# Half-row maximum tiles in pairs, after the four scores of a chunk, in a fused eight-block transformer kernel on one Trainium2 core

## The reference

```
x = x + slot_attention(layernorm(x))       # 4 heads, 64 slots, causal
x = x + mixture_of_low_rank_experts(layernorm(x))
x = x + polar_attention(layernorm(x))      # 16 heads of 8: "L0_attn_b"
x = x + mixture_of_low_rank_experts(layernorm(x))
x = x + distance_attention(layernorm(x))   # 16 heads of 8: "L1_attn_a"
x = x + squared_relu_ffn(layernorm(x))
x = x + gated_attention(layernorm(x))      # 16 heads of 8: "L1_attn_b"
x = x + squared_relu_ffn(layernorm(x))
```

```
# polar: q and k are turned into (magnitude * cos, magnitude * sin), 16 numbers per head
scores = einsum(q_embed, k_embed) / D ** 0.5;             attn = softmax(scores); out = attn @ v
# distance: queries and keys are the same Q
scores = -(|q|^2 - 2 q.q' + |q'|^2) * inv_sqrt_dk;        attn = softmax(scores); out = attn @ Q
# gated: a Gaussian window of learned centre P and width Z is added to the scores
scores = einsum(q, k) / sqrt(D) - (j - P) ** 2 * 2 / Z ** 2;  probs = softmax(scores); ctx = probs @ v
```

## Time and profile before

| | us |
|---|---|
| median of 3 runs | 2174.99 |
| lowest and highest run | 2159.97, 2195.99 |
| the profiled execution | 2177.36 |
| its span, first to last instruction | 2175.6 |
| TensorE busy (share of the span) | 1776.5 (82%) |
| VectorE busy | 1266.6 (58%) |
| ScalarE busy | 1311.8 (60%) |
| GpSimd busy | 337.1 (15%) |
| mean granted TensorE clock | 0.894 |

### The profile page before, as it was taken

The page is one execution under the profiler, slowest core; times in us unless marked ns, Lnnn a source line. Parts: engine busy times, 40 slices in busy tenths (PEclk is TensorE's granted clock), DMA queues, the critical chain, the costliest instruction groups (busy, mean ns, idle before and its releaser), DMA issues. The chain is left out here.

```text
span 2175.6 us, 30769 instructions
## 1 busy us (share of the span) xinstructions
PE 1776.5 (82%) x10152; PEld 806.9 (37%) x10152; DVE 1266.6 (58%) x2573; ACT 1311.8 (60%) x2250; POOL 337.1 (15%) x627
## 2 busy tenths in 40 slices
PE   1789985751999999978299888868762899999989
PEld 1476764640233333357111222225441233333347
DVE  2577776765888888745400000014555788888833
ACT  0456463762577777756256888846653377777764
POOL 0334231420000000023000000012330000000043
PEclk9999996975799999989656999989995799999999
DMA  3000000024222222100221222100223211111101
GB/s 92 0 2 1 1 1 1 30 87 140 69 71 67 69 69 66 46 1 26 54 41 32 44 42 47 32 1 15 73 73 130 63 54 56 51 58 52 45 1 40
DMA packets 122379, 100.25 MB, mean 46 GB/s; under 512 B 22586, under 2 KB 121591, under 8 KB 122221
## 3 DMA queue, kind: packets, MB, share of 16 engines
q1 hardware_dynamic: 122221, 98.27, 16.3%
HBM read 63.73 MB, written 34.47 MB: 45 GB/s over the span
## 5 line engine op out<-in xcount | busy, mean ns | idle before, releaser
L1654 ACT ACTIVATE a_probs<-a_ps_s 128x512 f32<-128x512 f32 (+1 forms) x1280 | 788.4, 688 | 416.8 <-PE a_ps_s L1581 416.0
L1682 DVE TENSOR_REDUCE a_minus_max<-a_ps_r 128x1 f32<-128x512 f32 x1024 | 634.0, 682 | 76.5 <-PE a_ps_r L1588 76.4
L1581 PE MATMUL a_ps_s<-a_q_stack,a_k_stack 98*128 98x512 bf16 (+2 forms) x1536 | 540.8, 398 | 38.0 <-DMA a_k_stack<-n_parts 33.3
L1588 PE MATMUL a_ps_r<-a_k_stack,a_q_stack 96*128 96x512 bf16 (+1 forms) x1024 | 403.0, 397 | 89.7 <-DMA a_k_stack<-k_parts 89.3
L1597 PE MATMUL a_ps_pv<-a_probs,a_v_ones 128*16 128x512 f32 x3072 | 429.5, 626 | 38.5 <-ACT a_ctxT L1645 37.7
L1581 PEld LDWEIGHTS a_ps_s<-a_q_stack,a_k_stack 98*128 98x128 bf16 (+2 forms) x1536 | 140.8, 99 | 441.1 <-ACT a_probs L1654 178.6
L1692 DVE RECIPROCAL a_inv<-a_ps_r 128x16 f32<-128x16 f32 x96 | 24.7, 258 | 406.2 <-PE a_ps_r L1605 406.2
L1588 PEld LDWEIGHTS a_ps_r<-a_k_stack,a_q_stack 96*128 96x128 bf16 (+1 forms) x1024 | 101.3, 99 | 207.6 <-issue 93.4
L1556 POOL CAST a_max_parts<-a_minus_max 128x16 bf16<-128x16 f32 x64 | 12.7, 198 | 751.0 <-DVE a_minus_max L1682 751.0
L1597 PEld LDWEIGHTS a_ps_pv<-a_probs,a_v_ones 128*16 128x16 f32 x3072 | 55.9, 95 | 186.1 <-ACT a_probs L1654 121.4
L1549 POOL COPY a_v_ones<-vtok 128x128 f32<-128x128 f32 x96 | 28.1, 293 | 349.8 <-PE a_ps_pv L1597 349.8
(11 more groups left out here) (346 smaller groups left out, 2564.1 us busy)
## 6 DMA issues: line engine op xcount, KB each, us to landing
a_q_stack<-q_parts SPq DMA_DIRECT2D x768, 32.0 KB
a_k_stack<-k_parts SPq DMA_DIRECT2D x576, 32.0 KB
g_parts<-d_p_curve_parts SPq DMA_DIRECT2D x8, 1152.0 KB, 4.9
q_parts<-d_p_q_parts SPq DMA_DIRECT2D x8, 768.0 KB, 3.6
k_parts<-d_p_k_parts SPq DMA_DIRECT2D x8, 768.0 KB, 3.6
q_parts<-d_p_q_parts SPq DMA_DIRECT2D x16, 384.0 KB, 2.9
a_k_stack<-q_parts SPq DMA_DIRECT2D x192, 32.0 KB
a_q_stack<-g_parts SPq DMA_DIRECT2D x192, 32.0 KB
```

What stands on the lines that cost most here:

```text
L1581: last = pe.matmul(ps_s[i % PAIRS][:, j, :], k_stack[m % SLOTS][:, h, c * P:(c + 1) * P], q_stack[m % SLOTS][:, h, :], start=True, stop=True)
L1588: pe.matmul(to[:, :], q_stack[n % SLOTS][0:rows, h, t * P:(t + 1) * P], k_stack[n % SLOTS][0:rows, h, :], start=True, stop=True).then_inc( ...
L1654: act.activation(probs[(NT * m + c) % PROBS][:, WIDE * part:WIDE * (part + 1), :], ps_s[i % PAIRS][:, :, :], ACT.Exp).then_inc(exp_done, 1)
L1682: dve.tensor_reduce(minus_max[n % 2][:, k:k + 1], ps[:, :], AX.X, ALU.max, negate=True).then_inc(bank_free, 1)
```

## The change

`tile` now contracts over the three largest products of parts only (48 rows in a3, 60 in a7). The rows of the stacks are laid out so that these lie in partitions 0 to 63 for the even heads of a group and in 64 to 127 for the odd heads, and the other three products in the other half; the two maximum rows come behind (`max_at`). A tile reads its own half (`part`), and `ORDER` alternates between an even and an odd head. A score still contracts over all rows (114 in a3, 126 in a7, among them rows that are zero on one side), and the maximum that is taken off it comes from the shorter product. In each chunk TensorE first issues the four scores and then the four tiles.

With the new layout come: stores in several pieces (`STORES` counts them): 6 for each split of d3, 3 and 3 and 7 in d7, each 128 rows of 1 KB or less, into tensors ordered by head; loads of up to 96 KB instead of 32: 12 per group in a3, 24 in a7, 14 as before in a5; loads split in queries and keys; a wait for each slot of its own (`filled`) instead of `zeroed`; the fills spread over GpSimd (`q_stack`), VectorE and, in a7, ScalarE, and the key loads of group 0 issued by ScalarE; in a5 the copy of `ps_pv` done by VectorE instead of ScalarE; gate rows of 512 KB instead of 108 KB; two instead of three buffers of the norm in the slot stage.

```diff
@@ -1074,13 +1077,14 @@
-                    for split, to in zip(prep.split, (sv.q_parts, sv.k_parts)):
+                    for split, to, places in zip(prep.split, (sv.polar_q, sv.polar_k), (Q_PLACE, K_PLACE)):
                         sp.wait_ge(split.lo_ready, b + 1)
-                        wait_ge(sp, split.stored, 16 * b)
-                        sp.dma_start(to[b].rearrange("i c r t -> r (i c) t"),
-                                     split.parts[b % 2][:, :, :, :].rearrange("p i c t -> p (i c) t")).then_inc(split.stored, 16)
+                        wait_ge(sp, split.stored, split.STORES * b)
+                        for i in range(3):
+                            for c in range(2):
+                                sp.dma_start(to[b, :, places[i], c * DH:(c + 1) * DH, :], split.parts[b % 2][:, i, c, :]).then_inc(split.stored, 16)
...
-def attention_phase(nc, sv, tag, rows, loads, ones_from=0, with_max=False, fixed=None):
+def attention_phase(nc, sv, tag, loads, rows=0, first=0, second=0, fixed=None):
...
+    with_max = first > 0
     LAG = 2 if with_max else 0
+    max_at = 64 + first
...
+    ORDER = [(2 * pair + parity, t) for pair in range(GH // 2) for t in range(NT) for parity in range(2)]
+    ONES = float(np.array([0x3F803F80], np.uint32).view(np.float32)[0])
...
                 for n in range(N):
                     b, g = divmod(n, NG)
+                    sp.wait_ge(filled[g], FILLS)
                     wait_ge(sp, scores_done, UNITS * (n - SLOTS + 1))
-                    for src, dst in loads(b, g, q_stack[g], k_stack[g]):
+                    queries, keys = loads(b, g, q_stack[g], k_stack[g])
+                    for src, dst in queries:
                         sp.dma_start(dst, src).then_inc(loaded[g], 16)
+                    if n > 0:
+                        for src, dst in keys:
+                            sp.dma_start(dst, src).then_inc(loaded[g], 16)
                     if with_max and n >= 2:
                         max_to_stack(n - 2)
...
             def _(pool):
+                for u in range(SLOTS):
+                    pool.memset(q_stack[u][:, :, :].bitcast(F32), 0.0 if with_max else ONES).then_inc(filled[u], 1)
...
-                pe.wait_ge(zeroed, 1)
+                pe.wait_ge(bank_zeroed, 1)
...
-                def tile(n, k):
-                    h, t = divmod(k, NT)
-                    to = bank(("tile", n, k))
-                    pe.matmul(to[:, :], q_stack[n % SLOTS][0:rows, h, t * P:(t + 1) * P], k_stack[n % SLOTS][0:rows, h, :],
+                def tile(n, i):
+                    h, t = ORDER[i]
+                    part = slice(64 * (h % 2), 64 * (h % 2) + first)
+                    to = bank(("tile", n, i))
+                    pe.matmul(to[:, :], q_stack[n % SLOTS][part, h, t * P:(t + 1) * P], k_stack[n % SLOTS][part, h, :],
                               start=True, stop=True).then_inc(bank_full, 1)
 
                 def pv(m, c):
@@ -1620,10 +1639,11 @@
                     if with_max and m >= 0:
                         pe.wait_ge(rows_loaded, 16 * (m + 1))
                     for c in range(NT):
-                        for i in range(PER):
-                            if m >= 0:
+                        if m >= 0:
+                            for i in range(PER):
                                 unit(m, PER * c + i)
-                            if tiles:
+                        if tiles:
+                            for i in range(4):
                                 tile(n, 4 * c + i)
                         if with_max and c == 0 and 1 <= s <= N:
                             turn_max(s - 1)
...
+                for u in range(SLOTS):
+                    if fixed is not None:
+                        act.activation(k_stack[u][0:all_rows, 1:GH:2, :], fixed[0:all_rows, 1, :].unsqueeze(1).to_broadcast([all_rows, GH // 2, T]),
+                                       ACT.Copy).then_inc(filled[u], 1)
+                    if u == 0:
+                        act.wait_ge(filled[0], FILLS)
+                        for src, dst in loads(0, 0, q_stack[0], k_stack[0])[1]:
+                            act.dma_start(dst, src).then_inc(loaded[0], 16)
...
                         if part == 0:
                             wait_ge(act, pv_done, NT * m + c - PROBS + 1)
                         act.activation(probs[(NT * m + c) % PROBS][:, WIDE * part:WIDE * (part + 1), :], ps_s[i % PAIRS][:, :, :], ACT.Exp).then_inc(exp_done, 1)
-                        if v == PER and m >= 1:
+                        if with_max and v == PER and m >= 1:
                             evacuate(m - 1)
-                evacuate(N - 1)
+                if with_max:
+                    evacuate(N - 1)
 
...
+                for u in range(SLOTS):
+                    if fixed is not None:
+                        last = dve.tensor_copy(k_stack[u][0:all_rows, 0:GH:2, :], fixed[0:all_rows, 0, :].unsqueeze(1).to_broadcast([all_rows, GH // 2, T]))
+                    elif with_max:
+                        dve.memset(k_stack[u][32:64, :, :].bitcast(F32), 0.0)
+                        last = dve.memset(k_stack[u][96:all_rows, :, :].bitcast(F32), ONES)
+                    else:
+                        last = dve.memset(k_stack[u][32:rows, :, :].bitcast(F32), ONES)
+                    last.then_inc(filled[u], 1)
+                    if u == 0:
+                        dve.memset(ps_pv[:, :], 0.0).then_inc(bank_zeroed, 1)
...
-                def reduce_tile(n, k):
-                    ps = full(("tile", n, k))
-                    if k == 0:
+                def reduce_tile(n, i):
+                    ps = full(("tile", n, i))
+                    k = ORDER[i][0] * NT + ORDER[i][1]
+                    if i == 0:
                         wait_ge(dve, parts_ready, n - 1)
...
+
+                def evacuate(m):
+                    dve.wait_ge(pv_done, NT * m + NT)
+                    if m >= 2:
+                        dve.wait_ge(bank_full, nth["ctx", m - 2] + 1)
+                    dve.tensor_copy(ctxT[m % 2][:, :], ps_pv[:, :]).then_inc(ctxT_ready, 1)
...
+                        if not with_max and c == 0 and s >= 1:
+                            evacuate(s - 1)
                         if c == 2 and s - LAG >= 1:
                             normalise(s - LAG - 1)
+                if not with_max:
+                    evacuate(N - 1)
...
+def split_loads(q, k, b, g, parity, q_stack, k_stack, first_at, second_at):
+
+    rows = q.shape[3]
+    own, heads = slice(parity, GH, 2), slice(g * GH + parity, (g + 1) * GH, 2)
+    first, second = 64 * parity + first_at, 64 * (1 - parity) + second_at
+
+    def of(parts, i, n):
+        return parts[b, heads, i:i + n, :, :].rearrange("h i r t -> (i r) h t")
+
+    queries = [(of(q, 1, 2), q_stack[first:first + 2 * rows, own, :]), (of(q, 2, 1), q_stack[first + 2 * rows:first + 3 * rows, own, :]),
+               (of(q, 0, 3), q_stack[second:second + 3 * rows, own, :])]
+    keys = [(of(k, 0, 1), k_stack[first:first + rows, own, :]), (of(k, 0, 2), k_stack[first + rows:first + 3 * rows, own, :]),
+            (of(k, 0, 3), k_stack[second:second + 3 * rows, own, :])]
+    return queries, keys
...
+    attention_phase(nc, sv, "a3", l0b_loads(sv), first=6 * DH, second=6 * DH)
     distance_phase(nc, sv, "d5", sv.l0b_w[:, 3, :])
-    attention_phase(nc, sv, "a5", 6 * DH + 6, l1a_loads(sv), ones_from=32)
+    attention_phase(nc, sv, "a5", l1a_loads(sv), rows=6 * DH + 6)
```

159 lines of the change are left out of this document (80 added, 79 removed).

## The result

The kernel after takes 2182.55 us (median of 20 executions, 2164.48 to 2194.30), the kernel before on the same chip 2169.15 (20 executions, 2148.79 to 2224.92). The ratio is 1.0084, 95% interval 1.0055 to 1.0112: 18 us slower, 12 to 24 by the interval. The forecast was 9 us faster. Seven of before's 20 executions, those more than 1.5% above its fastest, count as slow and are left out of the ratio; by the medians of all 20 the difference is 13 us. The difference is under 2% as forecast, but of the other sign, and the interval does not reach 1. The profiled execution of after took 2178.74 us, with a span of 2176.6.

A forecast was written before the change was run, and what follows sets the result against it. TensorE's order of issue was taken to bound a3 and a7, its wait for ScalarE's copy a5. 2177.4 + 53 - 39 - 41 + 8 + 10 = 2168.4, less 2.4: 2166 us, range 2125 to 2228.

The forecast's parts named there:

- 1 to 3, steady a3 and a7: a3 and a7: scores first, tiles in overlapping pairs, one more layout change per chunk: +0.89 us per group, +53 us.
- 4, copy in a5: a5: PV bank copy on VectorE shrinks TensorE's wait from 1.26 to about 0.05 us: -39 us, bounds 0 and -45.
- 5, starts: Starts of a3, a5, a7: slots load once filled, ScalarE issues group 0's keys; gains 11.9, 17.6, 11.8: -41 us.
- 6, stores: d3 and d7 stores in pieces: +0.8 x 6, and 3 us at stage ends: +8 us, bounds 0 and +25.
- 6, loads in a7: Steady a7: SyncE's 24 loads per group instead of 20 take 8.2 us of a 12.8 us group, hidden.
- 7, clock in a3 and a7: a3 and a7: one group more each at the low clock, each dearer by 5 us: +10 us, bounds -10 and +64.
- the gain of the tiles is spent here: a3 and a7 chunks: score 4 starts at +1.08 instead of +1.31, but nothing else is done in that wait.
- A: a3 and a7: tile pairs don't overlap, +133 instead of +53: 2246 us; chance 0.15.
- B: Layout switch free (-21), no extra low-clock time (-10): 2135 us, lower if a5's clock rises early; chance 0.22.
- C: a3 and a7 stay at the low clock as a5 did: 2220 us; chance 0.12.
- that estimate: Layout change as a full drain, 0.16 us instead of 0.09: 240 chunks add 17 us, time about 2183.

The follow-up runs named there:

- b_a5dve: Kernel before with only a5's copy of the PV bank moved to VectorE: ratio 0.9781 to before, a5 316.2 us against 380.2.
- a_a5act: Kernel after with a5's copy of the PV bank back on ScalarE: ratio 1.0323 to before, a5 346.1 us against after's 292.1.
- a_pk7: Kernel after with a7's six key loads per group issued by GpSimd instead of SyncE: ratio 1.0065 to before, a7 445.0 us.
- b_pieces: Kernel before with only the d3 and d7 stores split in pieces, to the old places: ratio 1.0028 to before, d3 161.7, d7 241.2 us.
- a_flat3: Kernel after with each d3 store written to one plain 128 KB stretch instead of by heads: ratio 1.0023 to before, d3 157.5 us.
- a_serial: Kernel after with four tiles of one half in a row, so none pair: ratio 1.0416 to before, group 14.25 us.
- a_twos: Kernel after with the order two scores, one pair of tiles, two scores, one pair: ratio 0.9806 to before, a3 group 11.46 us.

## Why the prediction was wrong

The forecast was 9 us faster, the kernel 18 slower. By the forecast's own items:

| item | forecast | runs |
|---|---|---|
| 1 to 3, steady a3 and a7 | +53 | +64: 60 x (12.97 - 11.90) |
| 4, copy in a5 | -39 | -47 (b_a5dve); -52 (a_a5act against after) |
| 5, starts | -41 | -38: 9.4, 16.9 and 11.2 |
| 6, stores | +8 | +40: d3 +18.9, d7 +21.3 |
| 6, loads in a7 | 0 | +3 to +8 (a_pk7) |
| 7, clock in a3 and a7 | +10 | about 0 |

The last column sums to +17 to +27; the kernel measured +18, 12 to 24. The +40 does not hang on one pair of profiles: averaged over the runs above that leave d3 or d7 alone, each of the two stages is 20 us longer with after's stores. The parts explain the whole within what single profiles and the two ratios can tell, no closer.

**The step that failed is item 6, stores in pieces.** It took "Six issues bring the last 1.7 us later", from an issue price of 0.34 us, and "+0.8 x 6, and 3 us at the two ends of stages (SyncE has no other work queued there)". All three were off:
- The price. 0.34 us is the issue of a load in a3's rows. A store into a plain 128 KB stretch is 0.47, and into the new layout by heads 0.62 (b_pieces, a_flat3). Six take 3.7 us. The forecast priced a layout by the issues of another layout. With the landing of 2.3 us the last store is done 1.9 us later than before (5.55 against 3.61), not 0.8; six times that is 11.6, and ScalarE's six waits grew by 11.4 (27.3 to 38.7).
- The stage. d3's waits for stores were counted and d7's were not. ScalarE waits there too, for q 11.5 us in before, 24.9 in after.
- The ends. SyncE does have other work queued there: the stores of the last two batches, q, k and, in d7, the curves: in d7 20 issues in a row from 1627.15 to 1639.91, in d3 24 from 521.63 to 536.92. VectorE's idle time before the first fill grew from 7.06 to 12.39 us at a3 and from 10.79 to 13.91 at a7: 5.3 and 3.1 us, where 3 us stood for both ends.

Waits for stores and ends give 18 of the 18.9 us of d3 and 17 of the 21.3 of d7.
So the bound of +25 was too low as well. This is the largest miss and enough to turn the sign: with +40 in its place the forecast is 23 us above before instead of 9 below. The other misses nearly cancel (steady +11, loads +3 to +8, starts +3, copy -8 to -13, clock -10); that they do is luck.

**Items 1 to 3** were right in mechanism: score 4 at +1.08 released by ScalarE, pairs in 0.22 (a_serial), a change of layout 0.09 to 0.10. Of the miss of 0.18 us per group, 0.13 is in chunk 0, 3.73 against 3.60 us, and the rest in the plain chunks, 2.92 against 2.90: TensorE reacts to VectorE 0.22 us after the reduce, where 0.09 was taken. The sentence "the gain of the tiles is spent here" is what a_twos shows: two tiles laid under that wait bring a group to 11.46.

**Item 4** was right in the group's time and wrong in "In steady a5 (warm, with gaps of 1.26 us) ... the clock did not fall". It fell in the profile of before itself: the granted clock is 0.69 over 1400 to 1405 us, in a group of 11.30 us. The forecast let a5 end at "some 1412"; it ended at 1439.9. In other executions of the same stage the clock fell every third group. So the copy's removal had a gain that was not counted. Its own sum was also off by 0.8 us: 27 x 1.26 and 5 x 0.84 are 38.2, not 39.

**Item 5** held within 4 us. **Item 6's "that is hidden"** for SyncE in a7 counted issues at 0.34 us: 8.2 us of a group. Its steep rows cost 0.48 each, the round trip of the maximum 1.5 us on the same queue was left out, and the sum is 12.14. **Item 7** asked for a group more at the low clock; the clock was up by 575 and 1684, 26 and 31 us after the first matmul against 28 and 22 in before: no whole group more.

**Rivals.** A (no overlap) is refuted by the four tiles in 0.61 us and by a_serial: undoing the overlap costs 3.3%. B was right that the clock takes no time more, and wrong on the switch, which costs 0.10 us. C did not happen. The rival that did, stores of more than their price on ScalarE's path, was held as an item with a bound and not as a rival.

By the Trainium skill, TensorEngine Tiling (Array Packing), Key Properties, changing the tiling mode drains TensorE. The trace shows 0.32 us for a step into or out of the half-row tiles against 0.22 without. A wait to the end of a record would make it 0.38, and that estimate was 17 us over the forecast; the measured step, 0.01 us above the 0.09 taken, is worth about 2 of them.
